# A conditioned residual block and a tanh recurrence on one core: first loads reordered, Wh in its own buffer, W2 tiles multiplied in pairs, chunk 0 dealt anew

## The reference

```python
# x (16, 512, 512), cond (16, 512), all float32
c = layernorm(cond) * gamma + beta
h = gelu(c @ W1 + bias1)                    # W1 512 x 512
w = h @ W2 + bias2                          # W2 512 x 16384 (33.5 MB), one set of factors per batch row
a1, b1, a2, b2 = split(w, 4) as (16, 512, 8)
u   = x @ a2                                # rank 8, per batch row
mid = gelu(x @ down + u @ b2.T)
v   = mid @ b1
x1  = x + (x + mid @ up.T + v @ a1.T)       # 2 x + out
# then a recurrence over the second axis, 512 steps
xW = x1 @ Wx + b
h_t = tanh(xW_t + h_(t-1) @ Wh)             # h_0 = cond
y  = x1 + h
```

## Time and profile before

| | |
|---|---|
| runs | 1255.58, 1256.99, 1260.54 us |
| the profiled execution | 1258.02 us, of which the span from first to last instruction 1256.3 us |
| PE busy | 1206.2 us (96%) |
| DVE busy | 914.0 us (73%) |
| ACT busy | 627.6 us (50%) |
| POOL busy | 280.2 us (22%) |
| setup, 0 to 140.9 us | PE 107.24 us busy, DMA share 0.86, 299 GB/s |
| steps, from 140.9 us | 1115.4 us; PE 1098.92 us busy, DMA share 0.18 |

### The profile page before, as it was taken

The page is one execution under the profiler, slowest core; times in us unless marked ns, Lnnn a source line. Parts: engine busy times, 40 slices in busy tenths (PEclk is TensorE's granted clock), DMA queues, the critical chain, the costliest instruction groups (busy, mean ns, idle before and its releaser), DMA issues.

```text
span 1256.3 us, 49350 instructions
## 1 busy us (share of the span) xinstructions
PE 1206.2 (96%) x20408; PEld 988.1 (79%) x20408; DVE 914.0 (73%) x3675; ACT 627.6 (50%) x2433; POOL 280.2 (22%) x523
## 2 busy tenths in 40 slices
PE   6778999999999999999999999999999999999996
PEld 5345788888888888888888888888888888888764
DVE  4444577878777787878787787878787777877564
ACT  2122455555555555555555545555555555554442
POOL 0000122222222222222222222222222222222111
PEclk9799999999999999999999999999999999999998
DMA  7998211312121211212121112213121211001022
GB/s 236 396 409 271 32 20 19 53 19 45 28 36 25 35 32 27 45 20 48 24 41 30 31 26 36 36 19 53 19 44 28 38 31 32 11 14 25 2 36 35
DMA packets 284078, 75.63 MB, mean 60 GB/s; under 512 B 273072, under 2 KB 273088, under 8 KB 283856
## 3 DMA queue, kind: packets, MB, share of 16 engines
q1 hardware_dynamic: 277488, 71.89, 24.4%
q10 hardware_dynamic: 6368, 0.60, 0.4%
HBM read 55.68 MB, written 16.78 MB: 58 GB/s over the span
## 4 chain that ended last, share of the span: by engine, by line
PE 89%; DMA 5%; ACT 2%; DVE 2%; SPq 1%; issue 1%; ACTq 0%; DVEq 0%; POOLq 0%; POOL 0%
PE bulk L949 44%; PE rec L965 32%; PE bulk L938 5%; PE bulk L952 5%; DMA work<-in_L_cond_W_dram 4%; ACT hf L607 1%; PE bulk L927 1%; SPq L447 1%; DVE z L830 1%; ACT rec L547 1%; PE bulk L887 1%; DMA hf<-in_L_cond_b_dram 0%; DVE work L797 0%; DVE wx_s L669 0%; ACT work L580 0%
## 5 line engine op out<-in xcount | busy, mean ns | idle before, releaser
L965 PEld LDWEIGHTS rec<-hs,wh_s 128*128 128x128 f16 x16352 | 442.7, 96 | 128.8 <-DVE hs L838 125.7
L607 ACT ACTIVATE hf<-z,scl 128x32 f32<-128x32 f32 x1024 | 273.9, 315 | 484.7 <-DVE z L830 480.2
L965 PE MATMUL rec<-hs,wh_s 128*128 128x32 f16 x16352 | 493.4, 177 | 6.9 <-ACT rec L547 6.9
L502 POOL TENSOR_TENSOR work<-work,hf 128x64 f32<-128x64 f32 x512 | 278.8, 544 | 966.4 <-DVE hs L838 966.4
L830 DVE TENSOR_REDUCE z<-rec 128x32 f32<-128x96 f32 x1022 | 231.1, 256 | 113.1 <-PE rec L965 99.7
L835 DVE TENSOR_SCALAR hs<-hf 128x32 f16<-128x32 f32 x1024 | 181.6, 177 | 105.9 <-ACT hf L607 105.9
L838 DVE SCALAR_TENSOR_TENSOR hs<-hf,hs 128x32 f16<-128x32 f32 x1024 | 197.3, 193 | 35.3
L949 PE MATMUL bulk<-act_x,down_s 128*128 128x512 f32 x768 | 219.0, 408 | 2.8 <-ACT work L580 2.8
L949 PE MATMUL bulk<-mid_s,up_s 128*128 128x512 f32 x768 | 217.6, 406 | 0.0
L949 PE MATMUL bulk<-act_s,wx_s 128*128 128x512 f32 x768 | 207.4, 407 | 0.0
L547 ACT ACTIVATE rec<-work 128x32 f32<-128x32 f32 x1022 | 183.7, 210 | 0.0
(11 more groups left out here) (105 smaller groups left out, 751.2 us busy)
## 6 DMA issues: line engine op xcount, KB each, us to landing
work<-in_L_cond_W_dram SPq DMA_DIRECT2D x33, 1024.0 KB, 9.0
work<-in_x_dram SPq DMA_DIRECT2D x256, 64.0 KB, 3.3
out_dram<-work SPq DMA_DIRECT2D x248, 64.0 KB, 2.4
work<-in_L_cond_base_up_dram SPq DMA_DIRECT2D x1, 1024.0 KB, 7.8
work<-in_L_cond_base_down_dram SPq DMA_DIRECT2D x1, 1024.0 KB, 10.6
work<-in_L_cond_Wh_dram SPq DMA_DIRECT2D x1, 1024.0 KB, 13.0
work<-in_L_cond_Wx_dram SPq DMA_DIRECT2D x1, 1024.0 KB, 9.2
out_dram<-work ACTq DMA_DIRECT2D x8, 64.0 KB, 3.2
```

The source lines that it names most:

```text
L502: nc.gpsimd.tensor_tensor(xs, xs, hf[:, t % 4], ALU.add).then_inc(sum_done, 1)
L607: nc.scalar.activation(hf[:, t % 4, half], z[:, half], ACT.Tanh, scale=inv).then_inc(tanh_done, 1)
L965: last = nc.tensor.matmul(R[fo][:, m, 0:PARTS, :], wh_s[:, q, k, n * P:(n + 1) * P], hs[:, k, :, :], start=(m == k == q == 0), stop=(k == ...
```

## The change

- SP loads x for chunk 0 right behind up, without a wait, then down, Wh and the W2 entries. W1 moves to work slot 5, Wh gets a buffer of its own. The transposes of x wait for `hT_mm` in place of `wh_split`.
- All four parts of up are turned and split in one go (the fourth in a bank of `rec`); then x is transposed and cast ("slot -1"), and only then down is cast and split, and Wh reduced.
- The first state moves from slot 1 to 0; Wh's casts from slots 2 and 3 to 4 and 12; Wx's from 28 and 29 to 29 and 30.
- `row(i-1)` and `row(i)` both run at odd i, one right behind the other.
- Chunk 0's pieces get other slots, out and xw other item orders and other PSUM banks (`FIRST_OUT`, `FIRST_XW`). DVE evicts two of the four xW tiles of chunk 0.
- Chunk 1's early slots on ACT and DVE run after slot 38 and 39 (before: 35 and 39).
- TensorE gets 16 and 8 more warming transposes, behind the state's and the condition's transposes.

```diff
@@ -36,14 +36,16 @@
 BANK_OUT = (2, 3, 1, 2)
 BANK_XW = (4, 5, 1, 3)
 BANK_ROW = 4
-BANK_UP = (3, 2, 1, 3)
+FIRST_OUT = (2, 3, 1, 0)
+FIRST_XW = (4, 5, 2, 3)
+BANK_UP = (3, 2, 1)
 BANK_COND = 5
 BANK_W1 = 4
 BANK_SCALE = 0
 COLG = 4
 BANK_IDLE = 0
 SQ = 32
-WARM_MM = 12
+WARM_MM = (12, 16, 8)
 
 
...
@@ -69,6 +71,15 @@
+def first_out_items(kt):
+
+
+
+    main = [[(m, k, p) for k in range(kt) for p in range(len(PASSES))] for m in range(kt)]
+    low = [[(m, g, -1 - w) for g in range(GROUPS) for w in (HI, LO)] for m in range(kt)]
+    return main[0] + main[1] + main[2] + low[0] + main[3][:6] + low[1] + main[3][6:] + low[2] + low[3]
+
+
 def first_xw_items(kt):
 
...
@@ -76,9 +87,9 @@
-    early, late = (0, 1), (2, 3)
-    items = [it for pair in (early, late) for k in range(kt - 1) for it in part(pair, k)]
-    return items + part(early, kt - 1) + part(late, kt - 1)
+    early, late = (2, 3), (0, 1)
+    order = [(early, 0), (early, 1), (late, 0), (late, 1), (early, 2), (late, 2), (late, 3), (early, 3)]
+    return [it for pair, k in order for it in part(pair, k)]
 
 
@@ -114,11 +125,10 @@
 
 
 STREAM = 40
-UP3_AT, STATE_AT, SCALE_AT = 1, 1, 2
-WH_HI_AT, WH_LO_AT = 2, 3
-WX_HI_AT, WX_LO_AT = 28, 29
-NEXT_ACT = {35: range(-21, -9), 39: range(-9, 0)}
-NEXT_DVE = {35: range(-21, -9), 39: range(-9, 0)}
+STATE_AT, WMAX_AT, SCALE_AT = 0, 1, 2
+WH_HI_AT, WH_LO_AT = 4, 12
+WX_HI_AT, WX_LO_AT = 29, 30
+NEXT_AT = {38: range(-21, -9), 39: range(-9, 0)}
 
@@ -169,7 +179,7 @@
-        wh_f = work[:, RING + 1, :].rearrange("p (k n) -> p k n", k=KT)
+        wh_f = sb("wh_f", [P, KT, D])[:]
...
-        w1_f = work[:, RING, :].rearrange("p (k n) -> p k n", k=KT)
+        w1_f = work[:, RING + 1, :].rearrange("p (k n) -> p k n", k=KT)
...
@@ -389,15 +403,16 @@
 
 
 
-        FIRST = {"u": (10,) * KT, "v": (25,) * KT,
-                 "mid": at_slots(first_items(KT), (7, 8, 9, 11, 13, 14, 17, 19, 21), (6, 6, 6, 6, 6, 6, 12, 12, 4)),
-                 "out": at_slots(first_items(KT), (23, 24, 26, 26, 27, 28, 30, 32, 33, 34, 36),
-                                 (6, 6, 6, 6, 6, 6, 4, 4, 4, 12, 4)),
-                 "xw": at_slots(first_xw_items(KT), (33, 35, 37, 37, 38, 38, 39, 39), (6,) * 8),
-                 "xt": (5, 5, 6, 6), "xhi": (5, 6, 6, 7), "xlo": (6, 6, 7, 7),
-                 "ub": 11, "ua": 12, "usel": 13, "ulo": 14, "gel": (17, 18, 19, 22), "mlo": (18, 19, 20, 22),
-                 "vb": 25, "va": 26, "vsel": 27, "vlo": 28, "x1": (31, 33, 34, 37), "x1hi": (32, 33, 34, 37),
-                 "x1lo": (32, 34, 35, 38), "xwev": (40,) * KT}
+        STEADY["out_banks"], STEADY["xw_banks"] = BANK_OUT, BANK_XW
+        FIRST = {"u": (9,) * KT, "v": (25,) * KT,
+                 "mid": at_slots(first_items(KT), (4, 5, 5, 7, 13, 15, 18, 19, 21), (6, 6, 6, 6, 6, 6, 12, 12, 4)),
+                 "out": at_slots(first_out_items(KT), (23, 24, 26, 27, 28, 29, 30, 30, 31, 32, 33, 35),
+                                 (6, 6, 6, 6, 6, 6, 4, 6, 4, 6, 4, 4)),
+                 "xw": at_slots(first_xw_items(KT), (33, 34, 35, 35, 36, 36, 38, 38), (6,) * 8),
+                 "xt": (-1, -1, -1, -1), "xhi": (-1, -1, -1, -1), "xlo": (-1, -1, -1, 1),
+                 "ub": 9, "ua": 10, "usel": 11, "ulo": 13, "gel": (18, 18, 19, 22), "mlo": (18, 19, 20, 22),
+                 "vb": 26, "va": 27, "vsel": 28, "vlo": 29, "x1": (31, 32, 34, 36), "x1hi": (31, 32, 34, 36),
+                 "x1lo": (32, 33, 35, 37), "xwev": (40,) * KT, "out_banks": FIRST_OUT, "xw_banks": FIRST_XW}
 
@@ -446,14 +461,13 @@
                 for i in range(P // SQ):
                     sp.dma_start(xn[i * SQ:(i + 1) * SQ, :, k, :], rows(x, c, k)[i]).then_inc(x_in[k], 16)
 
-            for e in range(HALVES + 3):
+            load(UP_ENTRY)
+            for k in range(KT):
+                load_x(0, k)
+            load(DOWN_ENTRY)
+            sp.dma_start(wh_f, wh.rearrange("(k p) n -> p k n", p=P)).then_inc(wh_in, 16)
+            for e in range(W2_ENTRY, HALVES + 3):
                 load(e)
-                if e == DOWN_ENTRY:
-                    sp.dma_start(wh_f, wh.rearrange("(k p) n -> p k n", p=P)).then_inc(wh_in, 16)
-                if e == RING - 1:
-                    sp.wait_ge(hT_mm, 1)
-                    for k in range(KT):
-                        load_x(0, k)
 
...
@@ -574,18 +586,21 @@
+                    if n == 0 and m % 2:
+                        continue
                     act.wait_ge(xw_mm, n * KT + m + 1)
                     if m == 0:
                         need(act, y_out, IN_OUT * (n - 1))
-                    nc.scalar.activation(xw[:, n % 2, m], bulk[:, BANK_XW[m], :], ACT.Identity,
+                    nc.scalar.activation(xw[:, n % 2, m], bulk[:, at["xw_banks"][m], :], ACT.Identity,
                                          bias=bs[:, m:m + 1], scale=fwd).then_inc(xw_done, 1)
 
+            dense_slot(0, -1)
+            arrived(act, DOWN_ENTRY)
+            nc.scalar.copy(down_s[:, HI], down_f).then_inc(w_hi, 1)
             for i in range(STREAM + 1):
                 for n in range(LAST + 1):
                     if i == 2 * n + 3:
                         factor_high(n)
-                if i == UP3_AT:
-                    up_high(KT - 1)
                 if i == WH_HI_AT:
                     act.wait_ge(scl_done, 1)
...
@@ -744,8 +730,8 @@
-                if n == 0:
-                    dve.wait_ge(wh_split, 1)
+                if n == 0 and k == 0:
+                    dve.wait_ge(hT_mm, 1)
...
@@ -782,13 +768,19 @@
+                for m in tile_at(at["xwev"], r) if n == 0 else ():
+                    if m % 2:
+                        dve.wait_ge(xw_mm, m + 1)
+                        nc.vector.tensor_scalar(xw[:, 0, m], bulk[:, at["xw_banks"][m], :], fwd, bs[:, m:m + 1],
+                                                ALU.mult, ALU.add).then_inc(xw_done, 1)
+
             def turn_y(c, k):
 
...
@@ -813,7 +835,7 @@
...
@@ -982,8 +1009,10 @@
-                    if i in mid[2] and m in (0, 2):
-                        need(pe, xw_done, (n - 1) * KT + 3 + m // 2)
+                    if n == 1 and i in mid[2] and m == 1:
+                        pe.wait_ge(xw_done, KT)
+                    if n > 1 and i in mid[2] and m in (0, 2):
+                        pe.wait_ge(xw_done, (n - 1) * KT + 3 + m // 2)
                     if i in mid[2] and m == KT - 1:
                         pe.wait_ge(gel_done, n * KT + 1)
@@ -1004,13 +1033,15 @@
-                    if i in out[2] and m == KT - 1:
+                    if n == 0 and i in out[2] and m == KT - 1:
+                        pe.wait_ge(rank_sum, 2)
+                    if n and i in out[2] and m == KT - 1:
                         pe.wait_ge(x1_done, n * KT + 1)
                     if p == -1 and m == k == 0:
                         pe.wait_ge(rank_done, 2 * n + 2)
                     if n == 0 and p == -1 and k == 0:
                         pe.wait_ge(fac_split, 3 * KT + m + 1)
-                    dense(out, i, BANK_OUT, up_s, mid_s, a1_s, out_mm)
+                    dense(out, i, sched(n)["out_banks"], up_s, mid_s, a1_s, out_mm)
                 for i in xw_plan[1].get(r, ()):
                     m, k, p = xw_plan[0][i]
@@ -1018,22 +1049,23 @@
-                        pe.wait_ge(x1_done, m + 1)
-                    if p == 0 and m == 0:
+                        pe.wait_ge(x1_done, 2)
+                    if p == 0 and m == (0 if n else 2):
                         pe.wait_ge(x1lo_done, n * KT + k + 1)
-                    dense(xw_plan, i, BANK_XW, wx_s, act_s, None, xw_mm)
+                    if n == 0 and k == KT - 1 and p == 0 and m == 0:
+                        pe.wait_ge(x1lo_done, KT)
+                    dense(xw_plan, i, sched(n)["xw_banks"], wx_s, act_s, None, xw_mm)
 
             for i in range(STREAM + 1):
-                if i < HALVES:
+                if i % 2 and i < HALVES:
+                    row(i - 1)
                     row(i)
                 if i % 2 and 0 <= i // 2 - 1 <= LAST and W2_TILES[i // 2 - 1][0] in (0, 3):
                     turn(i // 2 - 1)
-                if i == UP3_AT:
-                    pe.wait_ge(up_split, 1)
-                    turn_up(KT - 1)
-                if i == STATE_AT:
+                if i == WMAX_AT:
                     pe.wait_ge(wmax_done, 1)
                     nc.tensor.transpose(bulk[0:1, BANK_SCALE, 0:P], wmax[:, 2:3], ident[:]).then_inc(wmax_tr, 1)
+                if i == STATE_AT:
                     pe.wait_ge(wh_in, 16)
                     for m in range(KT):
                         last = first_state(m)
```

More of the change, by code:

```diff
@@ L312, in turned, with up_bank @@
             return rec[:, n % 2, 512 - GROUPS * P:512]
+        def up_bank(k):
+            return bulk[:, BANK_UP[k], :] if k < len(BANK_UP) else rec[:, 0, :]
         def turned_count(n):
@@ L528, in up_high @@
                 act.wait_ge(up_tr, k + 1)
-                nc.scalar.copy(up_s[:, HI, k], bulk[:, BANK_UP[k], :]).then_inc(up_hi, 1)
```

(44 more changed lines are left out.)

6 lines of the change are left out of this document (3 added, 3 removed).

## The result

The changed kernel takes 1262.01 us (median of 13 runs) against 1256.99: the ratio is 1.0032, with a 95% interval of 1.002 to 1.0044, so it is slower, by 4 us as the ratio has it and by 5 as the medians have it. The forecast was 1257.2, range 1248 to 1262.

The account below looks back on a forecast made before the run. The W2 stream's DMA bounds 52.9 to 112.0 us of the setup; the TensorE-busy recurrence is almost untouched. Terms −1.0 + 5.9 − 3.1 − 1.6 = +0.2 gave 1258.2 us, or 1257.2 as a median; range 1248 to 1262.

Parts of the forecast that it names:

- The last half: Last W2 half, whose load waits for Wx's split: landing 11.6 us after entry 32's, not 5.7; +5.9 us, bounds +3 and +6.5.
- part 4: From the last W2 half's landing to z: 22.7 us in place of 25.8, −3.1 us, including +1.5 for a low clock.
- The tail: Last W2 half's landing to z: six of 12 matmuls done ahead, two evictions for four; −3.1 us, bounds −5.2 and −1.
- the first step: From z to the first step: chunk 1's first matmuls run under the evictions; −1.6 us, bounds −2 and 0.
- The head: Loads before the full stream, x sent behind W1 and up: entry 10 lands at 51.8, −1.0 us, bounds +1.1 and −4.3.
- part 2: W2 stream with paired rows and wide matmuls: late-freed slots stay hidden, 0 us, bounds −0.5 to +1.
- The forecast alone: The summed terms without the rivals: 1257.2 us as a median, range 1253 to 1261, chance 0.54.
- x is hidden: Rival in the setup's first loads: DMA takes x behind W1 and up, entry 10 lands at 48.5; 1253.9 us, chance 0.15.
- clearly faster: Rival: early loads gain 4.3 us and Wx's cast gets ahead of rows 29, so no late load; 1248.0 us, chance 0.22.
- The clock in the stream: Rival in the W2 stream: pairs lengthen TensorE's idle pieces and its clock falls; +6 to +11, say 1265 us, chance 0.09.
- the sign that I had named: Sign of a wrong forecast: a granted TensorE clock under 1 between 55 and 105 us.

## Why the prediction came out as it did

- **The last half (+5.9): right in mechanism and, in the profile, in size (+5.9).** Wx's slots are worth 7.1 and 6.3 us on the changed kernel, 7.0 with the first state moved, 6.5 with single rows, and 6.6 the other way on the kernel before. That is a little more than the wait, as behind it the changed kernel's tail begins at half clock (1.2 us, which I had priced in part 4).
- **The tail (−3.1) and the first step (−1.6): right**, measured −4.1 and −1.7 in this profile; no run took them out one by one. The forecast end of the chain, two evictions on ACT behind its copy for chunk 1, is what the trace shows.
- **The head (−1.0): wrong, +4.2, outside my bound of +1.1.** The steps up to the issues held: Wh at 27.7 (27.0 forecast), the first state at half clock for 7.01 us, row 0 at 34.7 (34.0), entry 6 issued at 36.70 (36.0), entry 10 issued at 46.67 (46). The step that failed is the landing: I let an entry land 5.16 us after its issue with nothing in front, and 2.57 behind another. By that rule the real issues (36.70, 38.41, 42.42, 44.09) would have landed entry 9 at 50.2. The chain of the changed kernel has:

```profile
44.09 9.53 DMA work<-in_L_cond_W_dram
```

It landed at 53.62, 4.6 later than in the kernel before (row 7 at 49.0); entry 10, queued behind it, I had at 51.8. While rows 0 to 5 freed the slots in bursts, the DMA engines moved 322 GB/s and not 411 (their share of busy time was 0.93 all the same): over 16.6 us that is 3.6 us of stream. So my bounds, made of best and worst issue times, were too narrow: behind a ring refilled late, entries didn't land at the full rate. Why they didn't stays open. Nor is it always 3.6: the five other traces with x first and the first state in slot 0 moved 327 to 365 GB/s there, and had row 23 at 92.70 to 93.77, 1.4 to 2.4 us behind the kernel before, where the changed kernel's profile has it 3.7 behind. The last 0.5 us of the +4.2 came in the stream from row 23 to row 29 (18.7 us for 18.2), inside part 2's bounds.
- **The median.** The sum of this execution's terms is +4.3, its time 1263.06 against 1258.02 (+5.0), the medians +5.0 and the ratio +4.0. The median of 1262.01 stands on the range's upper edge of 1262 (1261.0 by the ratio). That it isn't further out is luck: the head missed by 5.2 us, outside every bound I gave it, and the tail gave 1.0 of them back. "The forecast alone" I had at 1253 to 1261.
- **The rivals.** "x is hidden" and "clearly faster" fell: x's hole moved, and Wx's cast didn't get ahead. The clock in the stream was 0.94 in 52.9 to 112.0, not 1.00: the sign that I had named. But the stream moved 397 GB/s there, for 395 before, so it had no price to speak of; the slower outcome came from the head and the last half.

## What to carry to other kernels

When a cast or a split frees the buffer of a load, count what stands ahead of it in its engine's own order: one slot later put it behind a transpose that hangs on two more pieces of the stream, and that cost 6 to 7 us. Moving a load forward is paid by the loads behind it; look first for what waits for those, and put the ones with long chains of work behind them (here down and Wh) ahead of the one with slack (x); here that gave 1.2 to 2.1 us at row 23. And price a late-refilled ring by a stretch of the trace in which it runs dry, not by the full rate.

## What the runs showed that I had not expected

- Pieces of 64 KB in rows of 128 bytes cost 0.6 to 0.8 us each of the stream's time also between 1 MB loads (2.4 to 3.1 us for four), with the DMA engines' share at 1.00 and 1.03.
- An engine that issues DMAs itself can stand in the issues: ACT for 23.5 us in 16 of them.
- The same head, instruction for instruction, reached row 23 at 95.05, 93.00 and 93.58 in three executions. The last had TensorE at half rate in rows 2 and 3 like the first, so the clock doesn't explain the difference. Before a loss at the head is put down to the clock, a second trace of the same instructions is worth having.
